# GpSimd may gather three groups of rows ahead of VectorE's sums in place of two

## The reference, cut to what matters

```
xl = x @ Wl + bl ; xr = x @ Wr + br                # 6250 x 128 each, 4 heads (1 head in the third layer)
e_feat = leaky_relu(xl[src] + xr[dst], 0.2)        # one row per edge
logits = einsum('ehc,hc->eh', e_feat, att)
a = exp(logits - segment_max(logits, dst)[dst])    # softmax over the edges of one destination
a = a / segment_sum(a, dst)[dst]
out = segment_sum(xl[src] * a, dst) + bias         # then layer norm and relu
```

## Time and profile before

| | us |
|---|---|
| runs (3) | 8517.47, 8529.99, 8535.05; median 8529.99 |
| the profiled execution | 8491.84 |
| its span, first to last instruction | 8489.9 |
| mean granted TensorE clock | 0.679 of full speed |
| VectorE busy | 5222.4 (62%) |
| TensorE busy | 4879.8 (57%) |
| GpSimd busy | 4740.8 (56%) |
| ScalarE busy | 4307.0 (51%) |

### The profile page before, as it was taken

One profiled execution on the slowest core, in us unless ns is written; L12 is line 12 of the kernel. 1 busy time (PEld: TensorE's weight loads), 2 busy tenths in 40 slices (PEclk: granted clock), 3 DMA queues, 4 the chain that ended last, 5 costly groups with the idle time before them and its releaser, 6 DMA issues.

```text
span 8489.9 us, 109176 instructions
## 1 busy us (share of the span) xinstructions
PE 4879.8 (57%) x24176; PEld 4286.7 (50%) x24176; DVE 5222.4 (62%) x16308; ACT 4307.0 (51%) x10681; POOL 4740.8 (56%) x4843
## 2 busy tenths in 40 slices
PE   4666666666666655555555555545555555544446
PEld 3565656565656544444444444444444444444444
DVE  5555565656565656766666667655555555555556
ACT  3444444444454545555555555545555555555546
POOL 3555555555555545666666666656666666666640
PEclk7666666666666666766767767666666666666666
DMA  5333333333333322322322323222222222222221
GB/s 147 94 100 91 96 97 97 97 96 97 96 98 95 98 67 74 79 76 76 77 75 77 82 77 78 76 66 72 77 71 71 72 72 72 76 73 72 72 61 50
DMA packets 460163, 697.83 MB, mean 82 GB/s; under 512 B 140781, under 2 KB 330019, under 8 KB 460101
## 3 DMA queue, kind: packets, MB, share of 16 engines
q0 software_dynamic: 154752, 327.15, 16.9%
q1 hardware_dynamic: 305349, 370.00, 14.2%
HBM read 638.95 MB, written 57.76 MB: 82 GB/s over the span
## 4 chain that ended last, share of the span: by engine, by line
PE 33%; issue 27%; DVE 22%; another core or an unknown queue 7%; ACT 6%; POOL 3%; DMA 2%; SPq 0%; DVEq 0%; ACTq 0%; POOLq 0%
PE PS L791 14%; PE PS L763 10%; PE PS L783 6%; DVE z L1186 3%; POOL xl_g L706 3%; DVE am L1193 3%; DVE msg L1285 2%; ACT distT L931 2%; ACT ST L936 2%; DVE relu_logit L1202 1%; ACT dist L906 1%; PE PS L749 1%; DMA xl_g<-xl_tab,edges 1%; DVE relu_logit L1205 1%
## 5 line engine op out<-in xcount | busy, mean ns | idle before, releaser
L706 POOL DMA_INDIRECT xl_g<-xl_tab,edges x4836 | 4740.0, 980 | 3485.8 <-DVE z L1186 1689.1
L763 PE MATMUL PS<-xr_w,ST 128*128 128x132 f32 x9672 | 2054.2, 373 | 2160.7 <-issue 1278.8
L763 PEld LDWEIGHTS PS<-xr_w,ST 128*128 128x128 f32 x9672 | 1778.9, 269 | 2455.4 <-issue 1735.2
L791 PE MATMUL PS<-msg,S 128*128 128x137 f32 x9672 | 1829.7, 352 | 936.8 <-issue 648.7
L791 PEld LDWEIGHTS PS<-msg,S 128*128 128x128 f32 x9672 | 1710.6, 257 | 1017.6 <-issue 1012.0
L1186 DVE TENSOR_TENSOR z<-PS,xl_g 128x528 f32<-128x528 f32 x1302 | 856.6, 658 | 1428.1 <-DMA xl_g<-xl_tab,edges 823.2
L906 ACT ACTIVATE dist<-node_row,neg_dst 128x128 f32<-128x128 f32 x4836 | 1534.5, 386 | 0.0
L931 ACT ACTIVATE distT<-dst_all,neg_node 128x512 f32<-128x512 int16 x1302 | 884.0, 679 | 1029.7 <-DVE neg_dst L1179 725.5
L909 ACT ACTIVATE S<-dist 128x512 f32<-128x512 f32 x1302 | 780.4, 599 | 839.9 <-remote 625.2
L1193 DVE SCALAR_TENSOR_TENSOR am<-z,att_relu 128x512 f32<-128x512 f32 x1302 | 860.8, 661 | 115.0 <-remote 94.1
L936 ACT ACTIVATE ST<-distT 128x512 f32<-128x512 f32 x1302 | 780.0, 599 | 42.6 <-ACT distT L931 1.4
(11 more groups left out here) (220 smaller groups left out, 3691.4 us busy)
## 6 DMA issues: line engine op xcount, KB each, us to landing
dst_all<-dst_short SPq DMA_DIRECT2D x186, 832.0 KB
xl_g<-xl_tab,edges POOLq DMA_INDIRECT x4836
ea<-edge_attr SPq DMA_DIRECT2D x124, 432.0 KB
ea<-edge_attr SPq DMA_DIRECT2D x62, 384.0 KB
xr_w<-xr_tab SPq DMA_DIRECT2D x186, 66.0 KB
dst_r<-dst_rows SPq DMA_DIRECT2D x186, 64.0 KB
node_row<-node_id SPq DMA_DIRECT2D x186, 64.0 KB
state<-t_new SPq DMA_DIRECT2D x126, 68.0 KB
```

Source lines behind the costliest of these rows:

```text
L706: pool.indirect_dma_start(xl_g[:, q, t, :], None, xl_tab[stage][:, :], bass.IndirectOffsetOnAxis(idx[:, q, t:t + 1], 0))\
L763: last = pe.matmul(zp[(q + g) % 3][:, n, :], ST[:, t, :], xr_w[:, q, :], start=True, stop=True)
L791: last = pe.matmul(agg_ps, S[:, q, t, :], msg[:, t, :], start=t == 0 and stage > 0, stop=t == TILES - 1)
```

## The change

One constant: the lead that GpSimd is allowed goes from two groups to three.

```
-BEHIND = 2
+BEHIND = 3
```

## The result

The changed kernel is slower. Its median is 8657.15 us (8643.62 to 8666.11, 4 runs), that of the kernel before in the same comparison 8523.73 (8509.83 to 8535.05, 4 runs): a ratio of 1.0156, with a 95% interval of 1.0143 to 1.0169. The forecast was 8430 us. The measured time lies just inside the stated range of 8270 to 8660, but on the other side of 8530 than was forecast. The profiled execution took 8643.62 us, 151.8 more than that of before.

A forecast was written before the change was run, and what follows sets the result against it. No engine was taken as the bound: the chain was TensorE 33%, "issue" 27%, VectorE 22%. Fewer long steps gave 100 us, other terms 0: 8530 - 100 = 8430 us, range 8270 to 8660.

The forecast's parts named there:

- z4 sorts the steps into short and long: Stages one and two: steps are long when z4 starts late after z0; an earlier z4 makes them short, saving 100 us.
- the mark of 18.5: Start of z4 in us after z0 from which long steps were found; the change would put z4 1.5 us below it.
- The term of 129, or 100, us: Stages one and two: 17 and 16 long steps becoming short would save 129 us; three quarters taken, 100 us.
- The excess of 4.5 us a long step: Stage one: a long step lasts 51.12 us against 46.59 for a short one, the difference to be saved.
- between -115 and +186 of gain: Stage three: an earlier z2 could gain 186 us or lose 115 us over 62 steps; taken as 0.
- z4's wait in stage two: Stage two: z4's 1.96 us wait for gathers goes, worth 0 to 122 us over 62 steps; taken as 0.
- GpSimd's idle time before its first gather behind z0: Sign expected in the profile after: near 5 us in stage one in place of 10.
- TensorE starts its sums too early: Slower rival: earlier messages 3 and 4 make stage two's short steps long, costing 152 us; 8625 to 8682 us; chance 0.29.
- The lead comes through: Faster rival: all bounded gains arrive, 408 us, giving 8122 us, or half of it, 8326; chance 0.14.
- The rival that leaned on the Trainium skill: No-change rival: stalls stay whatever z4 does, "issue" belonging to loop branches; 8530 us; chance 0.17 together with no effect.

The follow-up runs named there:

- lead2: The kernel before, lead of two groups, unchanged, run again on another chip with stalls: 8510.57 us.
- lead3: The changed kernel, lead of three groups against two, on the same chip with stalls as the repeat of the kernel before: 8672.27 to 8705.27 us, ratio 1.0209.
- lead3_c: The changed kernel, lead of three groups against two, once more on a further chip with stalls: 8657.94 us, ratio 1.0138.

## Why the prediction was wrong

**The step that failed** is "z4 sorts the steps into short and long", the whole of the 100 us. It took a coincidence in the trace of before for a cause. z4 came to 16.6 and 16.5 us after z0 in stages one and two, well below the mark of 18.5, and by z6 later than 31.5 us 14 and 10 of 54 steps are long, where 13 and 6 were; by their length, as the prediction counted, 14 and 15, where 13 and 11 were. The number of long steps didn't fall. The term of 129, or 100, us has 0 in its place. The excess of 4.5 us a long step wasn't to be had either: run `lead2` has one long step in stage one, and its steps take 47.4 us in the mean, against 47.5 with thirteen.

**What stood in its place.** The stall belongs to GpSimd's run of gathers, which the prediction never laid beside it, although it wrote that all groups behind group 2 "go out back to back". From z0+1.5 to z0+24.4 there are 18 of them, and TensorE's last stall ends 2.2 to 2.7 us behind their end (medians of stages one and two, leads 2 and 3). Lead 3 doesn't shorten that run. It moves four gathers out of its front (group 2 now goes out ahead of z0) and lets four of the next item in at its back: group 0 then waits for z4 in place of z5. In the traces of before and after, GpSimd gathers from z0+1.5 to 24.4 and from z0+1.8 to 24.9 in stage one. z6 therefore stays where it was, and even comes 0.5 us later in the short steps.

What does sort the steps is GpSimd's pause behind the 18th gather. In the five traces of the two kernels with stalls (before, `lead2`, after, `lead3`, `lead3_c`; 810 steps) z6 comes later than 31.5 us where that pause is under 2.4 us and sooner where it is longer, in 783 of them. In stage one of before it is 0.5 to 2.3 us in the thirteen long steps and 2.8 or more in the others; in the changed kernel, with z4 moved, 1.7 to 2.6 and 2.9 or more. After a short pause the stall goes on through the next four gathers. The pause isn't only a wait: in the step at 1253.32 of before, z5 is done at 1277.40, and GpSimd's next gather starts 3.6 us later. So GpSimd's own next instruction comes late too, and what sets the length of the pause there stays open:

```profile
1276.69 0.71 DVE L1186 TENSOR_TENSOR z<-PS,xl_g 128x528 f32<-128x528 f32 x1
...
1280.98 0.94 POOL L706 DMA_INDIRECT xl_g<-xl_tab,edges  x1 [3.46 <-remote]
```

**Where it got worse.** The run can go on from 18 to 22 gathers only if the `z` that it needs next is done at some z0+24.5. In before that is z5, and in after z5 too, for one group later. In stage three that decides it: z5 is now done in 52 of 54 steps, and in all of them the run goes on within 1 us; in before it is 47, of which 42 go on. In stages one and two it doesn't: in after z5 is done in time in 44 steps of each, and the run goes on in none and in 4. And TensorE, which in the step at 6433.23 stood waiting for message 3 until 22.6 us after z0, has it at 18 in the step at 6619.24 and takes its instructions singly from 19 on in place of 24. When it goes on, 20 rows of sums are left in place of 17 (means of the stage); its last sum starts 37.2 us after z0 in place of 35.5, and the step takes 42.4 us in place of 41.2. 62 x 1.2 = 74 of the 82 us of that stage. I had put 0 there, between -115 and +186 of gain; it was a loss inside that bound.

**z4's wait in stage two** was taken at 0 of a possible gain of 122, and that stage lost 57: its short steps take 41.4 us in place of 40.6, and the steps over 43 us are 15 in place of 11. That the first comes of the run's end being 0.3 us later fits, but no run shows it.

**Right**: that the waits of `z` for gathers would go, z4 at 16.5 to 17 us, nothing gained by it where z6 waits, and that the stall falls at a fixed distance from z0. Wrong in small: GpSimd's idle time before its first gather behind z0 was not halved in stage one; it is 10.9 us in the mean (11.0 before), since it goes out of credit at the border as before, one group later.

**The rivals.** *TensorE starts its sums too early* came nearest, with 8625 to 8682 against 8657, and in part by luck. Its mechanism is half of the truth, and in another stage: stage two cost 57 of its 152 us, and stage three, where it had put nothing, 82. *The lead comes through* is what happens without stalls: 7197 to 6929 is 268 us, within what the lead was bounded by. The rival that leaned on the Trainium skill, "Runtime: NRT & Kernel Launch", section on instruction fetch mechanics, put the "issue" to taken branches. No run here bears that out: with the same loops and half the gathers the stalls are gone.

**What is shown and what is not.** Shown: where there are stalls they need the full number of gathers; with leads 2, 3 and 5 they end some 2 to 3.5 us after a run; their end depends neither on how many sums TensorE has (stages one and two) nor on the load of the destinations; SyncE, which waits for nothing, is slowed with the others. That fits a lack of instructions, for TensorE's single matmuls too, and hardly a wait for data. Not shown: by what path GpSimd's gathers slow the other engines, whether their count, their bytes or the missing pauses decide, whether a long pause lets the engines recover or both follow from one cause, and why three chips of six are free of it. A kernel with all its gathers and pauses of 3 us put in between on purpose wasn't tried.

## What to carry to other kernels

When engines stand on "issue" in mid-step, lay the busy runs of every other engine beside the stall, GpSimd's above all, before sorting steps by what came late in them; a mark that separates good steps from bad ones can be an effect of the same cause. A longer lead for gathers is worth its time only if the engines behind it can use it: here it gave 3.7% or cost 1.4 to 2.1%, depending on where it ran. And where a kernel's time differs by 18% between chips, find out which kind a measurement was made on before trusting its sign. A row of additions that wait for nothing, on an engine that is otherwise idle, shows in the trace when instructions come late.

## What the runs showed of the hardware

- The same kernel took 7187 to 7200 us on three chips and 8491 to 8551 on three others, each used in one job, with the same instructions and data; with half the gathers it took 6442 to 6458 on either kind.
- Where there were stalls, TensorE and VectorE got single instructions 0.7 to 2.8 us apart late in an unbroken run of gathers, from some 14 to 22 us into it, and recovered 2 to 3.5 us after it; VectorE once stood for 17.4 us with its work ready, from 11 us into the run on. Where there were none, GpSimd gathered through two whole stages and nothing stalled.
- 64 additions to a semaphore on SyncE, which wait for nothing, took 3.9 us on a chip without stalls and 26.5 us on one with them, 0.7 or 1.4 us for each of those that were held up while GpSimd gathered.
- 12 tiles less of 26 in the sums went with a granted clock of 0.616 in place of 0.683 on the same chip, and brought no time.
